# A graph layer on one core: first target scores fetched one a period, feature sums and residual moved to TensorE and ScalarE

## The chip, the cores and the metric

One core of one Trainium2 chip runs the kernel. The metric is the device time of one execution in microseconds (us), median of three runs. One execution was also recorded by the hardware profiler; all durations below come from that one.

## What is computed

Cut to what matters. `x` is 6250 x 256 in fp32, `src` and `dst` are 106250 edges sorted by target.

```python
xn = layernorm(x)
x = x + gnn(xn, src, dst) + mix(xn)
x = x + ffn(layernorm(x))            # 8 experts, softmax gate

def gat_conv(x, W, al, ar, src, dst):          # gnn: twice, 8 heads x 64, then 1 head x 256
    feat = x @ W;  el, er = feat . al, feat . ar
    e = leaky_relu(el[src] + er[dst], 0.2)
    alpha = exp(e - max over dst) / sum over dst
    return sum over dst of alpha * feat[src]

def mix(x):                                     # linear attention, 8 heads of 32
    q, k, v = elu(x Wq) + 1, elu(x Wk) + 1, x Wv
    context, k_sum = k^T v, sum of k
    return (q context / (q k_sum)) @ Wproj + bproj
```

elu(u) + 1 is max(u, 0) + exp(-max(-u, 0)): a positive part and an exponential part. For the keys the kernel calls the sum of the two parts `kphi`.

## The kernel before

The program runs five passes one after the other: the node pass (normalise, project, write the table of rows for layer one), the index pass, the edge pass of layer one, the hidden pass (ELU and the second projection), and the edge pass of layer two. `edge_pass` is one function, called with `L1` and the side work `Mixing`, then with `L2` and the side work `Experts`.

**The edge pass** cuts the edges, in order of target, into 52 blocks of 16 steps of 128 edges; four blocks form a group (13 groups), and each of the 128 lanes walks 64 consecutive edges per group. For each step GpSimd's queue (POOL) issues an indirect DMA that gathers 128 rows of the source nodes (2080 bytes each in layer one), L1349. In layer one there are two buffers of 16 steps, so the gather of step g of block n waits until VectorE (DVE) has summed step g of block n-2. In layer two there are three buffers. ScalarE (ACT) scales four of the eight heads of a step (L1486, four instructions a step), DVE the other four in one instruction a block (L1430). Then DVE adds step after step to a running sum, L1463, one 128x512 instruction a step in layer one. Each waits for the step before it. The softmax weights of block n+1 (`head`, L1402 to L1421) are worked out by DVE ahead of step 12 of block n in layer one, ACT takes their exponential (L1477, L1479, semaphore `wr_ready`) behind its last step of block n, and DVE's L1430 of block n+1 waits for it. Two rings of sums are stored to memory by SyncE's queue (SP), 1 MB each, after steps 8 and 16. In block 0 of each group the tails of the lanes of the last group are joined (class `Tails`), which makes that block longer.

**The scores of the targets** (`er`) are loaded per group. The first edge of each lane has its score fetched by its own indirect DMA, `first_er(q)`, L1339: the one of group 0 at the start, the other twelve in a run in block `n == B` (block 2 in layer one, block 3 in layer two), one ahead of each step's gather. At the very start POOL fetches `er_ali`, waits until it has landed, writes it to `starts` (L1334), and only then issues `first_er(0)` and the first gathers. SP's loads of `er` wait for that write.

**The side work of layer one**, class `Mixing`, is hung on the steps of the edge pass. In blocks 0 to 25 (the first half) two tiles of 121 nodes a block, t0 and t1, are projected by TensorE (`project`, L975 and L978, into the PSUM tiles p_kv and p_q). ACT makes the exponential parts of keys and queries behind its steps 4 and 11 (`exponents`, L941 to L945, tile `low`). DVE copies the values (L876, `vext`), adds up the keys' parts (L878, `kphi`) and the queries' parts (L880, into `nd_feat`, semaphore `q_kept`) ahead of steps 6 and 13. TensorE adds keys times values to the context (`context`, L986). TensorE's order is written out in `tensor`: project t0, context t0, project t1, context t1. `project` of a tile waits for `q_kept` of the tile before it.

In blocks 26 to 51 (the second half) the queries are weighed by the context (`weigh`, L1000 and L1001), DVE divides ahead of steps 2 and 8 (`quotient`, L902 to L906), TensorE transposes the result (`turn_back`, L1008), ACT copies it behind its steps 4 and 10 (`turn`, L951), TensorE projects it (`output`, L1016 and L1018, semaphore `o_ready`), and DVE adds the input row x ahead of steps 6 and 12 (`residual`, L915). TensorE's order is weigh t0, turn back t0, output t0, weigh t1, turn back t1, output t1. SP stores the result and loads the row of two tiles later.

The POOL queue's order and its one wait, around which a part of the change is made:

```python
for n in range(NB):
    for g in range(G):
        if n == B and 1 <= g < Q:
            first_er(g)
        wait(pool, summed, (n - B) * G + g + 1)
        nc.gpsimd.indirect_dma_start(out=rows[:, n % B, g, :], ...)
```

## Time and profile before

| | |
|---|---|
| median of 3 runs | 3355.85 us (3355.46 to 3357.4) |
| the profiled execution's own time | 3355.96 us |
| its span, first to last instruction | 3353.5 us, so 2.5 us lie around it |
| busy: PE, DVE, ACT, POOL | 2061.7, 2423.0, 1879.5, 2147.9 us |
| share of busy time: PE, DVE, ACT, POOL | 61%, 72%, 56%, 64% |
| mean granted TensorE clock | 0.752 of full speed |
| edge pass of layer one | from about 303 to 1645 us |
| edge pass of layer two | from about 1920 us to the end |

The shares are averages over passes with different limits, so each pass is read on its own. Engines: PE is TensorE's matmuls, PEld its weight loads, DVE is VectorE, ACT is ScalarE, POOL is GpSimd, SP is SyncE. A clock of 1.0 is 2.4 GHz, 0.5 is 1.2 GHz. An idle time in a row is that of the engine just before the instruction, with what ended it. Most instructions overlap the next by a part of their duration, so the cost of one in a row of them is the distance from start to start. A matmul in fp32 is two instructions in the profile. Matmul rows name output, moving operand, and stationary operand in the order out<-moving,stationary. A row of busy time by stretch has the stretch from and to in us from the span's start, its length, the busy us (and instructions) of PE, PEld, DVE, ACT and POOL, the granted clock, the mean busy share of the 16 DMA engines, and the GB/s that they moved. A row of a timeline has the start, the us, engine, line, operation, tiles, shapes, how many were merged (xN), and in brackets the idle time before them with what ended it.

### The profile page before, as it was taken

How to read it: one execution, taken by the hardware profiler on the slowest of the kernel's cores; microseconds unless marked ns; L12 is line 12 of the kernel's file. 1: busy time of each engine (PE TensorE's matmuls, PEld its weight loads, DVE VectorE, ACT ScalarE, POOL GpSimd, SP SyncE). 2: the span in 40 equal slices, each digit the busy share in tenths (PEclk: the TensorE clock that was granted, in tenths of full speed). 3: DMA queues.
4: the chain of work that ended last, by engine and by line, in shares of the span. 5: the costliest groups of instructions: out<-in, count | busy, mean ns of one | idle time of the engine just before them, and what ended most of it. 6: DMA issues, size and time to landing. Idle time of an engine off the chain costs nothing. (4 is left out here: it accounts for less than half of the span.)

```text
span 3353.5 us, 33809 instructions
## 1 busy us (share of the span) xinstructions
PE 2061.7 (61%) x6977; PEld 1301.7 (39%) x6977; DVE 2423.0 (72%) x6006; ACT 1879.5 (56%) x6177; POOL 2147.9 (64%) x2067
## 2 busy tenths in 40 slices
PE   6800354455545544444456500389999999999999
PEld 5600233333323322332244300255555555555565
DVE  6881799999988888888778535566666676767632
ACT  3400687777877766676544322456566566656632
POOL 2326777767666767676277577777777777777300
PEclk9955666666665555555588855699999999999999
DMA  7512899999999999999665357666666666666400
GB/s 232 138 22 82 277 368 346 354 351 360 348 350 344 366 352 367 346 366 365 258 169 147 85 170 246 197 188 207 206 207 208 217 217 205 201 205 207 156 26 12
DMA packets 249060, 793.61 MB, mean 237 GB/s; under 512 B 72064, under 2 KB 120035, under 8 KB 222197
## 3 DMA queue, kind: packets, MB, share of 16 engines
q0 software_dynamic: 132448, 379.32, 36.3%
q1 hardware_dynamic: 86327, 391.15, 30.7%
q10 hardware_dynamic: 30078, 20.99, 2.5%
q8 instruction: 56, 0.92, 0.1%
q14 instruction: 151, 1.24, 0.1%
HBM read 414.03 MB, written 378.16 MB: 236 GB/s over the span
## 5 line engine op out<-in xcount | busy, mean ns | idle before, releaser
L1349 POOL DMA_INDIRECT e_rows<-scratch_table,k_src x1664 | 1716.4, 1031 | 643.9 <-issue 347.9
L1486 ACT ACTIVATE e_rows<-e_rows,e_wr 128x64 f32<-128x64 f32 (+1 forms) x4160 | 1186.2, 367 | 3.4
L1463 DVE SCALAR_TENSOR_TENSOR e_ring<-e_ring,e_kext,e_rows 128x512 f32<-128x512 f32 (+1 forms) x1560 | 958.8, 615 | 239.1 <-ACT e_rows L1486 151.1
L2123 PE MATMUL e_p_y<-e_wfo,e_h 128*121 128x256 f32 x1664 | 394.1, 392 | 41.4 <-DVE e_y L1885 41.3
L2123 PEld LDWEIGHTS e_p_y<-e_wfo,e_h 128*121 128x121 f32 x1664 | 314.5, 191 | 139.6 <-ACT e_h L2032 66.5
L2109 PE MATMUL e_p_b<-e_h,e_wf 128*128 128x484 f32 x832 | 359.7, 575 | 10.6 <-ACT e_h L2032 10.6
L2097 PE MATMUL e_p_a<-e_xt,e_wf 128*128 128x484 f32 x832 | 357.6, 573 | 0.7 <-ACT e_xt L2047 0.7
L2032 ACT ACTIVATE e_h<-e_p_a,e_shift,e_scale 128x484 f32<-128x484 f32 x208 | 155.3, 752 | 269.6 <-PE e_p_a L2097 269.6
L986 PE MATMUL e_p_c<-e_vext,e_kphi 121*128 121x129 f32 x208 | 63.9, 462 | 310.2 <-DVE e_kphi L878 310.2
L1885 DVE SCALAR_TENSOR_TENSOR e_y<-e_p_y,e_w,e_y 121x256 f32<-121x256 f32 x416 | 180.3, 475 | 102.4 <-PE e_p_y L2123 102.3
L1430 DVE TENSOR_TENSOR e_rows<-e_rows,e_shared 128x4096 f32<-128x4096 f32 x52 | 229.6, 4416 | 15.4 <-ACT e_wr L1479 15.4
L2109 PEld LDWEIGHTS e_p_b<-e_h,e_wf 128*128 128x128 f32 x832 | 154.3, 191 | 178.5 <-issue 171.3
L2097 PEld LDWEIGHTS e_p_a<-e_xt,e_wf 128*128 128x128 f32 x832 | 157.6, 191 | 146.4 <-issue 140.9
L1008 PE MATMUL e_p_q<-k_ident,e_low 121*128 121x121 f32 x104 | 34.5, 434 | 291.8 <-DVE e_low L906 291.8
L2032 ACT ACTIVATE e_h<-e_p_b,e_shift,e_scale 128x484 f32<-128x484 f32 x208 | 152.6, 749 | 87.9 <-PE e_p_b L2109 86.1
L975 PE MATMUL e_p_kv<-e_wkv,nd_feat 128*121 128x512 f32 x208 | 184.2, 1041 | 0.0
L986 PEld LDWEIGHTS e_p_c<-e_vext,e_kphi 121*128 121x128 f32 x208 | 48.5, 323 | 318.5 <-DVE e_kphi L878 318.5
L1008 PEld LDWEIGHTS e_p_q<-k_ident,e_low 121*128 121x128 f32 x104 | 16.2, 215 | 297.0 <-DVE e_low L906 297.0
L951 ACT COPY e_att_t<-e_p_q 128x242 f32<-128x242 f32 x52 | 18.8, 362 | 182.0 <-PE e_p_q L1008 182.0
L1682 PE MATMUL hi_p_f<-hi_w,hi_ht 128*121 128x272 f32 x416 | 120.2, 439 | 0.0
L1016 PE MATMUL e_p_c<-e_wproj,e_att_t 128*121 128x256 f32 x208 | 105.8, 662 | 18.1 <-ACT e_att_t L951 18.1
L218 POOL DMA_INDIRECT na_found<-in_dst,na_piece x52 | 54.8, 1054 | 94.7 <-DVE na_piece L270 94.7
(406 smaller groups left out, 3466.7 us busy)
## 6 DMA issues: line engine op xcount, KB each, us to landing
scratch_sums<-e_ring SPq DMA_DIRECT2D x104, 2112.0 KB
scratch_sums<-e_ring SPq DMA_DIRECT2D x104, 1032.0 KB
e_rows<-scratch_table,k_src POOLq DMA_INDIRECT x1664
scratch_table<-na_frow ACTq DMA_DIRECT2D x52, 245.8 KB
scratch_table<-hi_frow ACTq DMA_DIRECT2D x52, 124.8 KB
na_x<-in_x SPq DMA_DIRECT2D x13, 484.0 KB
...
```

What stands on the lines that cost most here:

```text
L975: nc.tensor.matmul(self.p_kv[0:BK, :], self.k.feat[:, t, kt, :], self.wkv[:, kt, :], start=kt == 0, stop=kt == 1)
L986: last = nc.tensor.matmul(self.p_c[:, m * (P + 1):(m + 1) * (P + 1)], self.kphi[:, m * P:(m + 1) * P], self.vext[:, m, :], start=False, st ...
L1349: nc.gpsimd.indirect_dma_start(out=rows[:, n % B, g, :], out_offset=None, in_=table, in_offset=bass.IndirectOffsetOnAxis(ap=k.src[:, n * G ...
L1430: c(nc.vector.tensor_tensor(v, v, broad(share(b)[:, AH:H, 1:G1].rearrange("p h j -> p j h"), dim), ALU.mult))
L1463: nc.vector.scalar_tensor_tensor(ring[:, i, j - c0, 0:W], prev, kext[:, 0, j + 1:j + 2], rows[:, rb, j, 0:W], ALU.mult, ALU.add).then_inc( ...
L1486: last = nc.scalar.activation(rows[:, rb, j, at], rows[:, rb, j, at], ACT.Copy, scale=wr[:, b, h, j + 1:j + 2])
L1682: last = nc.tensor.matmul(p_f[b][0:BK, 0:D + 16], ht[:, b, kt, :], w2[:, kt, :], start=kt == 0, stop=kt == 3)
L1885: last = nc.vector.scalar_tensor_tensor(y, self.p_y[bank][0:BK, i % 2 * D:(i % 2 + 1) * D], self.w[:, i, e:e + 1], y, ALU.mult, ALU.add)
L2032: self.nc.scalar.activation(h[:, e % 2, mt, :], p[mt][:, 0:GN], ACT.Relu, bias=self.shift[:, layer, 2 * e + mt:2 * e + mt + 1], scale=self ...
L2097: last = nc.tensor.matmul(self.p_a[mt][:, 0:GN], self.wf1[:, e, kt, mt * P:(mt + 1) * P], self.xt[:, kt, :], start=kt == 0, stop=kt == 1)
L2109: last = nc.tensor.matmul(self.p_b[mt][:, 0:GN], self.wf2[:, e, kt, mt * P:(mt + 1) * P], self.h1[:, e % 2, kt, :], start=kt == 0, stop=kt ...
L2123: last = nc.tensor.matmul(self.p_y[bank][0:BK, i * D:(i + 1) * D], self.h2[:, e % 2, kt, v:v + BK], self.wfo[:, e, kt, :], start=kt == 0, ...
```

## The change

Three parts.

- POOL's order, both layers: `first_er(0)` and two gathers are issued ahead of the wait for `er_ali` and its write to `starts`. The other twelve first scores are fetched one a group, at step 8 of block 1 of the group before.
- First half of layer one: DVE no longer copies the values nor adds the keys' parts. ACT copies the values (`vext`) and writes the keys' positive part (`kphi`, now without the exponential part), and `context` multiplies both parts, `kphi` and `low`, with the values: four matmuls for two. ACT releases the context (`phi_ready`) itself.
- Second half: TensorE adds the input row x by a product with the identity, ahead of the projection, into the same PSUM tile. ACT copies the result behind its steps 7 and 13, DVE has no `residual`.

```diff
     def features(self, dve, t):
         nc, k = self.nc, self.k
-        dve.wait_ge(self.projected, t + 1)
-        wait(dve, self.ctx_added, t)
         if t == NB - 1:
+            dve.wait_ge(self.ctx_added, t)
             nc.vector.tensor_scalar(self.vext[:, :, P:P + 1], k.iop[0:BK, :].unsqueeze(1).to_broadcast([BK, 2, 1]),
-                                    float(NODES - t * BK), None, ALU.is_lt)
-        nc.vector.tensor_copy(self.vext[:, :, 0:P], self.p_kv[0:BK, D:2 * D].rearrange("p (m v) -> p m v", m=2))
+                                    float(NODES - t * BK), None, ALU.is_lt).then_inc(self.masked, 1)
         dve.wait_ge(self.exp_ready, t + 1)
-        nc.vector.scalar_tensor_tensor(self.kphi[:, :], self.p_kv[0:BK, 0:D], 0.0, self.low[0:BK, 0:D],
-                                       ALU.max, ALU.add).then_inc(self.phi_ready, 1)
         nc.vector.scalar_tensor_tensor(k.feat[:, t, :, :].rearrange("p m v -> p (m v)"), self.p_q[:, 0:2 * BK], 0.0, self.low[:, D:D + 2 * BK],
                                        ALU.max, ALU.add).then_inc(self.q_kept, 1)

-    def residual(self, dve, t):
-        nc = self.nc
-        dve.wait_ge(self.o_ready, t + 1)
-        dve.wait_ge(self.x_in[t % 2], t // 2 * 16 + 16)
-        wait(dve, self.res_out[t % 2], t // 2 * 16)
-        nc.vector.tensor_tensor(self.res[:, t % 2, :], self.p_c[0:BK, 0:D], self.x[:, t % 2, :],
-                                ALU.add).then_inc(self.res_ready, 1)
+    def residual(self, act, t):
+        act.wait_ge(self.o_ready, t + 1)
+        wait(act, self.res_out[t % 2], t // 2 * 16)
+        self.nc.scalar.copy(self.res[:, t % 2, :], self.p_c[0:BK, 0:D]).then_inc(self.res_ready, 1)

     def exponents(self, act, t):
         nc = self.nc
         act.wait_ge(self.projected, t + 1)
+        wait(act, self.ctx_added, t)
         wait(act, self.q_kept, t)
         nc.scalar.activation(self.low[0:BK, 0:D], self.p_kv[0:BK, 0:D], ACT.Relu, scale=-1.0).then_inc(self.low_ready, 1)
         nc.scalar.activation(self.low[:, D:D + 2 * BK], self.p_q[:, 0:2 * BK], ACT.Relu, scale=-1.0).then_inc(self.low_ready, 1)
+        nc.scalar.copy(self.vext[:, :, 0:P], self.p_kv[0:BK, D:2 * D].rearrange("p (m v) -> p m v", m=2))
+        nc.scalar.activation(self.kphi[:, :], self.p_kv[0:BK, 0:D], ACT.Relu)
         act.wait_ge(self.low_ready, 2 * t + 2)
-        nc.scalar.activation(self.low[0:BK, 0:D], self.low[0:BK, 0:D], ACT.Exp, scale=-1.0)
         nc.scalar.activation(self.low[:, D:D + 2 * BK], self.low[:, D:D + 2 * BK], ACT.Exp, scale=-1.0
                              ).then_inc(self.exp_ready, 1)
+        nc.scalar.activation(self.low[0:BK, 0:D], self.low[0:BK, 0:D], ACT.Exp, scale=-1.0).then_inc(self.phi_ready, 1)

     def context(self, pe, t):
         nc = self.nc
         pe.wait_ge(self.phi_ready, t + 1)
+        if t == NB - 1:
+            pe.wait_ge(self.masked, 1)
         for m in range(2):
-            last = nc.tensor.matmul(self.p_c[:, m * (P + 1):(m + 1) * (P + 1)], self.kphi[:, m * P:(m + 1) * P],
-                                    self.vext[:, m, :], start=False, stop=False, skip_group_check=True)
+            for part in (self.kphi, self.low):
+                last = nc.tensor.matmul(self.p_c[:, m * (P + 1):(m + 1) * (P + 1)], part[0:BK, m * P:(m + 1) * P],
+                                        self.vext[:, m, :], start=False, stop=False, skip_group_check=True)

     def output(self, pe, t):
         nc = self.nc
+        wait(pe, self.res_ready, t)
+        pe.wait_ge(self.x_in[t % 2], t // 2 * 16 + 16)
+        nc.tensor.matmul(self.p_c[0:BK, 0:D], self.k.ident[0:BK, 0:BK], self.x[:, t % 2, :], start=True, stop=False)
         pe.wait_ge(self.att_kept, t + 1)
-        wait(pe, self.res_ready, t)
         for m in range(2):
             nc.tensor.matmul(self.p_c[0:BK, 0:D], self.att_t[:, m * BK:(m + 1) * BK], self.wproj[:, m, :],
-                             start=m == 0, stop=False)
+                             start=False, stop=False)

         @block.gpsimd
         def _(pool):
...
-            pool.wait_ge(ali_in, 16)
-            nc.gpsimd.indirect_dma_start(
-                out=starts, out_offset=bass.IndirectOffsetOnAxis(ap=k.ali_row[:, 0:1], axis=0),
-                in_=er_ali[:, 0:EW], in_offset=None, bounds_check=P * T - 1, oob_is_err=False).then_inc(ali_out, 16)
...
             first_er(0)
             for n in range(NB):
                 for g in range(G):
-                    if n == B and 1 <= g < Q:
-                        first_er(g)
+                    if n == 0 and g == 2:
+                        pool.wait_ge(ali_in, 16)
+                        nc.gpsimd.indirect_dma_start(
+                            out=starts, out_offset=bass.IndirectOffsetOnAxis(ap=k.ali_row[:, 0:1], axis=0),
+                            in_=er_ali[:, 0:EW], in_offset=None, bounds_check=P * T - 1, oob_is_err=False).then_inc(ali_out, 16)
+                    if n % PB == 1 and g == G // 2 and n // PB + 1 < Q:
+                        first_er(n // PB + 1)
                     wait(pool, summed, (n - B) * G + g + 1)
```

`Mixing.vector` loses its two calls of `residual`, `Mixing.scalar` has them behind steps 7 and 13; the semaphores of the first scores alternate by group (`er0_in[q % 2]`).

How the order moves. POOL at the start of the edge pass of layer one, before (e_er stands for the tile of the first scores, e_rows for that of the gathered rows):

```order
L1331 DMA e_er_ali<-scratch_er,k_ali_dst 13x8
L1334 DMA scratch_starts<-e_er_ali,k_ali_row 106496x8
L1339 DMA e_er<-scratch_er,k_dst 128x8
L1349 DMA e_rows<-scratch_table,k_src 128x520 x33
L1339 DMA e_er<-scratch_er,k_dst 128x8
```

and with the change:

```order
L1332 DMA e_er_ali<-scratch_er,k_ali_dst 13x8
L1336 DMA e_er<-scratch_er,k_dst 128x8
L1351 DMA e_rows<-scratch_table,k_src 128x520 x2
L1345 DMA scratch_starts<-e_er_ali,k_ali_row 106496x8
L1351 DMA e_rows<-scratch_table,k_src 128x520 x22
L1336 DMA e_er<-scratch_er,k_dst 128x8
L1351 DMA e_rows<-scratch_table,k_src 128x520 x64
L1336 DMA e_er<-scratch_er,k_dst 128x8
```

The write to `starts` has gone behind two gathers, and the first scores of the next groups come once in 64 gathers.

TensorE in one block of the second half, before (L1008 turns back, L1016 and L1018 are the output, L1000 and L1001 weigh the next tile):

```order
L1008 MATMUL e_p_q<-k_ident,e_low 128x121 x2
L1016 MATMUL e_p_c<-e_wproj,e_att_t 121x256 x2
L1018 MATMUL e_p_c<-e_bproj,e_one 121x256
L1000 MATMUL e_p_kv<-e_cbd,nd_feat 121x128
L1001 MATMUL e_p_kv<-e_ksum,nd_feat 121x4
```

and with the change:

```order
L1007 MATMUL e_p_q<-k_ident,e_low 128x121 x2
L1014 MATMUL e_p_c<-e_wkv,k_ident 121x256
L1017 MATMUL e_p_c<-e_wproj,e_att_t 121x256 x2
L1019 MATMUL e_p_c<-e_bproj,e_one 121x256
L999 MATMUL e_p_kv<-e_cbd,nd_feat 121x128
L1000 MATMUL e_p_kv<-e_ksum,nd_feat 121x4
```

A matmul of 256 columns (L1014; e_wkv is where the row x lies) stands between the transposes and the projection, ahead of the weighing of the next tile.

## Rows read from the trace of the kernel before

**Rows 1.** Busy time by stretch: first half, second half, layer two.
```profile
620.00:1000.00 380.00, 188.94 (x522) 117.45 (x520) 346.27 (x638) 299.29 (x1208) 269.50 (x245) 0.65 0.95 351
1080.00:1560.00 480.00, 227.16 (x652) 145.11 (x652) 423.12 (x821) 330.21 (x1365) 328.02 (x303) 0.51 0.96 361
2400.00:2770.00 370.00, 350.31 (x1161) 209.01 (x1160) 257.79 (x820) 225.12 (x516) 282.85 (x287) 0.98 0.68 209
```
**Rows 2.** Timeline of POOL, start of layer one (start, us, what, idle before).
```profile
303.77 0.90 POOL L1331 DMA_INDIRECT e_er_ali<-scratch_er,k_ali_dst  x1 [7.24 <-POOLq L114]
306.68 0.91 POOL L1334 DMA_INDIRECT scratch_starts<-e_er_ali,k_ali_row  x1 [2.01 <-DMA e_er_ali<-scratch_er,k_ali_dst]
352.84 0.94 POOL L1339 DMA_INDIRECT e_er<-scratch_er,k_dst  x1 [0.30 <-issue]
```
**Rows 3.** Timeline of DVE, same stretch: its waits for gathered rows.
```profile
358.65 0.39 DVE L1402 TENSOR_TENSOR e_z<-e_rows,e_er 128x128 f32<-128x128 f32 x1 [6.07 <-DMA e_rows<-scratch_table,k_src]
391.49 0.46 DVE L1402 TENSOR_TENSOR e_z<-e_rows,e_er 128x128 f32<-128x128 f32 x1 [10.22 <-DMA e_rows<-scratch_table,k_src]
```
**Rows 4.** Waits of POOL in layer two, 1900 to 3200: total, times, longest.
```profile
POOL e_rows L1349 <- issue: 190.4, 625, 0.3
...
POOL scratch_starts_b L1334 <- DMA e_er_ali<-scratch_er,k_ali_dst: 2.2, 1, 2.2
```
**Rows 5.** Busy time of blocks 12 and 14; sums of blocks 12-15 and 32-35.
```profile
645.72:672.15 26.43, 11.54 (x37) 7.34 (x37) 25.13 (x51) 22.50 (x92) 18.87 (x17) 0.69 0.94 336
...
695.78:719.83 24.05, 12.11 (x33) 7.56 (x32) 22.43 (x46) 19.20 (x79) 13.63 (x13) 0.64 0.86 322
...
sum 99.00, PE 50.23 PEld 31.30 DVE 90.20 ACT 78.31 POOL 67.57; mean PE 12.56 PEld 7.83 DVE 22.55 ACT 19.58 POOL 16.89
...
sum 102.79, PE 48.12 PEld 30.55 DVE 90.66 ACT 70.68 POOL 64.81; mean PE 12.03 PEld 7.64 DVE 22.67 ACT 17.67 POOL 16.20
```
**Rows 6.** Timeline of DVE, block 14.
```profile
706.65 0.40 DVE L876 COPY e_vext<-e_p_kv 121x256 f32<-121x256 f32 x1
...
707.30 0.40 DVE L880 SCALAR_TENSOR_TENSOR nd_feat<-e_p_q,e_low 128x242 f32<-128x242 f32 x1
...
715.77 0.75 DVE L1463 SCALAR_TENSOR_TENSOR e_ring<-e_ring,e_kext,e_rows 128x512 f32<-128x512 f32 x1 [0.83 <-ACT e_rows L1486]
...
717.42 2.49 DVE L1463 SCALAR_TENSOR_TENSOR e_ring<-e_ring,e_kext,e_rows 128x512 f32<-128x512 f32 x3
```
**Rows 7.** Timeline of TensorE, block 14.
```profile
707.44 1.23 PE L986 MATMUL e_p_c<-e_vext,e_kphi 121*128 121x129 f32 x4 [8.05 <-DVE e_kphi L878]
708.46 3.62 PE L975 MATMUL e_p_kv<-e_wkv,nd_feat 128*121 128x512 f32 x4
711.87 1.48 PE L978 MATMUL e_p_q<-nd_feat,e_wq 128*128 128x121 f32 x8
```
**Rows 8.** Timeline of ACT, block 14.
```profile
713.39 0.38 ACT L941 ACTIVATE e_low<-e_p_kv 121x256 f32<-121x256 f32 x1 [4.76 <-PE e_p_q L978]
...
714.69 3.91 ACT L1486 ACTIVATE e_rows<-e_rows,e_wr 128x64 f32<-128x64 f32 x16
```
**Rows 9.** Timeline of DVE, block 34.
```profile
1215.79 0.42 DVE L915 TENSOR_TENSOR e_wkv<-e_p_c,e_wkv 121x256 f32<-121x256 f32 x1 [0.97 <-PE e_p_c L1018]
1217.85 0.14 DVE L902 TENSOR_SCALAR e_den<-e_p_kv 121x8 f32<-121x8 f32 x1
```
**Rows 10.** Timeline of TensorE, block 34.
```profile
1212.55 2.06 PE L1016 MATMUL e_p_c<-e_wproj,e_att_t 128*121 128x256 f32 x4 [0.45 <-ACT e_att_t L951]
1214.55 1.21 PE L1018 MATMUL e_p_c<-e_bproj,e_one 1*121 1x256 f32 x2
1215.68 0.78 PE L1000 MATMUL e_p_kv<-e_cbd,nd_feat 128*121 128x128 f32 x2
...
1217.09 0.42 PE L1001 MATMUL e_p_kv<-e_ksum,nd_feat 128*121 128x4 f32 x2
```
**Rows 11.** Timeline of ACT, block 34.
```profile
1219.45 0.36 ACT L951 COPY e_att_t<-e_p_q 128x242 f32<-128x242 f32 x1 [0.82 <-PE e_p_q L1008]
```

14 lines of the change are left out of this document (7 added, 7 removed).

## The prediction

> **What bounds the kernel now.** I read the busy time by stretch first, to see which passes the change touches and what is near its limit there. In both halves of layer one DVE is busy 91% and 88% of the time and the DMA engines 95% and 96%, at 351 and 361 GB/s; TensorE has slack, and its clock stands mostly at its lower level, 1.2 GHz (granted 0.65 and 0.51) [rows 1]. In layer two neither is full. There POOL is: its waits are 625 gaps of 0.3 us with the releaser "issue", none longer, and one single wait of 2.2 us at the start [rows 4]; 287 indirect DMAs in 370 us are one each 1.29 us [rows 1]. So layer two costs what POOL has to issue, whatever the order.
>
> Then I read the blocks of layer one, which repeat in fours: 99.0 us in the first half, 102.8 us in the second [rows 5]. The same four blocks move some 34.7 MB and 37.1 MB (351 and 361 GB/s), and at a full share the engines would move 351/0.95 = 369 and 361/0.96 = 376 GB/s, so the transfers alone need 94.0 us and 98.7 us. That is a floor near by, but the view of waits names none of DVE in the two stretches that is for a transfer.
>
> Last I read the timelines, for what DVE waits for. In block 14 it is a loop over four engines. DVE adds the queries' parts (L880) and so releases `q_kept`; TensorE finishes context t0 and projects t1; ACT starts its exponents at 713.39, 5.69 us after L880 ended, and has waited 4.76 us for that [rows 6 to 8]. Four ACT instructions later come the rows, DVE waits 0.83 us for the first of them [rows 6], and ACT's weights for the next block are just ready when DVE gets there at 719.83 [rows 5]. The reader is to see that DVE is 91% busy and yet paced by this loop.
>
> **Part one, the order of POOL.** In layer one POOL waited 2.01 us for `er_ali` [rows 2]; with three indirect DMAs in between (1.25 us each) that has landed, and only the usual 0.3 us gap is left: -1.7 us, since DVE's first weights wait for the sixteenth gather. The twelve first scores stood in a run from 352.84 on [rows 2], each ahead of one gather, and DVE then waited 10.22 us for the rows of block 2 [rows 3]. Twelve less one at 1.25 us are 13.75 us, more than the wait, so it goes: -10.2 us. Next late would be DVE itself. SP's loads of `er` start 3 us later, hidden by the 16 gathers. The wait of 6.07 us in block 0 [rows 3] stays. In layer two the count of DMAs is the same and POOL never rests, so only the wait of 2.2 us, less its gap, is saved: -1.9 us. The run there cost DVE a wait too, but DVE only gets a lead that POOL takes back by 1.25 us a group. Bounds: -3.6 us if the rows of block 2 are late for another reason, -19.9 us if the wait in block 0 goes too. Sum: -13.8 us.
>
> **Part two, the first half.** From L876 to L880 in start times are two instructions, 0.65 us [rows 6]. They leave DVE twice a block: 1.3 us. But in blocks like 14 the loop decides:
> - L880 comes 0.65 us earlier: -0.65.
> - Context t0 leaves the way to project t1, since ACT now releases it long before. It stood there from 707.44 to 708.46, while `q_kept` came at 707.70, so 0.76 us [rows 6, 7]. Without its run-in TensorE may do the eight short products (1.48 us, some of them at 2.4 GHz) at 1.2 GHz throughout, up to 0.4 us more: I take -0.45.
> - ACT gets a copy and a relu between 713.39 and the rows at 714.69, where four take 1.30 us [rows 8]. Two more are 0.65 at most; less where the wait between relus and exponentials is now covered: +0.5. The row of ACT's added ones is that of its neighbours, as no row shows the copy from PSUM by itself.
> - The four rows behind them take ACT 3.91 us, 0.98 each [rows 8]; DVE takes 0.83 for a sum [rows 6]. So ACT leads the end of the block and DVE's second 0.65 us is mostly lost.
>
> That is -0.6 us for each of two blocks in four. In block 12 and its like the joining of the tails makes DVE's part longer (26.43 us) [rows 5] and ACT waits little: the full -1.3. In the last of four ACT keeps a copy of the sums after DVE's last step: -0.65 and a part of the second, -0.8. Four blocks: -3.3 us, to 95.7, above the 94 of the transfers. Blocks 3 to 25 are 23: 23/4 x 3.3 = **-19 us**. The doubled context (four fp32 products, 1.0 us more, TensorE idle 8.05 us before it [rows 7]) lies outside the loop. Bounds: 0, when ACT's two instructions cost 0.65 and TensorE gives nothing (the loop then still keeps -0.65 of DVE, which DMA at its floor could eat), and 5 us of four blocks down to the transfers' 94, -29.
>
> **Part three, the second half.** DVE loses `residual`: 0.34 us for t1, and for t0 the wait, 0.97 us in block 34 [rows 9]. But what follows it there is `quotient` t1 at 1217.85, and that needs the weighing of t1, which TensorE ended at 1217.51 [rows 9, 10]. So the wait was cover: DVE would only wait at L902 instead. And the identity product is put before it. Two passes of 256 columns cost what two of L1016's four do, 1.0 us of 2.0 [rows 10]; 0.45 us of it fits in the gap in which TensorE waits for ACT's copy [rows 10], so the weighing ends 0.55 us later, at 1218.1, and L902 0.3 us later. ACT's copy of the result (0.36, as [rows 11] by shape) waits for `o_ready` behind step 7, holds steps 8 to 10, and makes the turn of t1 some 0.5 us later than 1219.45, where ACT had 0.82 us of slack [rows 11]. The 0.34 us of t1 pays the 0.3 back. In the two blocks in four where the tails' products stand in that gap the identity product shows in full, +0.1 and +0.4. Four blocks: +0.5; over 26 blocks +3 us, and some of it comes back where the longer stretch of TensorE's work raises its clock. I take **0**. No row shows the product or the copy itself, so the bounds: -1.0 us a block (all DVE instructions and waits gone, down to the transfers' 98.7 us a four), -27 us, and +0.5 us a block, +13.
>
> **The sum** against the profiled execution's own 3355.96 us (0.1 above the median): -13.8 - 19 + 0 = -32.8, so **3323 us**.
>
> **Rivals.**
> - TensorE speeds up. For it: output and weighing, 4.96 us from 1212.55 to 1217.51, get the identity product where the gap was, and with the transposes ahead of it become one unbroken stretch of over 6 us [rows 10]; against it: the clock is 0.51 in a half that already has 4.96 [rows 1]. If it does, it is in the weighing, at the end of the stretch. Its 1.83 us (1215.68 to 1217.51) then halve, L902 comes 0.45 us earlier than before, and with the 0.34 that is -0.8 us x 26 = -21: 3302 us. Chance 0.2. The Trainium skill ("TensorE: Matmul & The Clock Gate", What's actually happening) says that activity releases the clock, the default being the lower one; by that rule the change would come out here, and the higher clock of the first half, where the unbroken stretch is 5.9 us (707.44 to 713.35) [rows 7], agrees.
> - DVE was the bound. Its instructions and its short waits all count: first half down to the transfers (23/4 x 5 = -29), second too (-27): 3356 - 14 - 56 = 3286 us. For it the 91%, against it the waits behind both. Chance 0.12.
> - Mixing gives nothing: ACT's two instructions at full price, TensorE's project slower by what the context left, and the +3 us of the second half. Then only POOL's order counts, 3342 to 3345 us. Chance 0.13. This is also the case that the moved work isn't the moved bound.
> - Slower. ACT and TensorE take turns in series in the second half: identity product 1.0, the wait for `o_ready` behind step 7 1.0 and the copy 0.36, all on the way to the turn of t1, less none: 2.4 us a block, +62, with -33 elsewhere: 3385 us. It decides from 1.3 us a block on (33/26). The 0.82 of ACT's slack [rows 11] speaks against it. Chance 0.04.
>
> **How the numbers follow.** The forecast has 0.5 with 3308 to 3340 as its own range (-29 or -9 in the first half, -8 to +10 in the second). Rivals: 0.2, 0.12, 0.13, 0.04, and 0.01 for none. From 3290 to 3343 leaves out the DVE rival, the slow one and a bit of the third. A measurement of this kernel can tell 0.2%, 6.7 us, from no change. Faster by more: 0.5 + 0.2 + 0.12 and most of 0.13, 0.93; within: 0.04; slower: 0.03.
>
> **What would show it.** The wait of 10.22 us gone and block 1 near 23 us instead of 33; four blocks of the first half near 95.7 us, with DVE still waiting for ACT; in the second half near 103, with a new wait of DVE at L902 for the weighing, 1 us or more, where that at L915 was; a clock above 0.6 there would be the first rival. Layer two from its start to its end shorter by 2 us alone. If DVE begins to wait for gathered rows in the middle of layer one, the transfers have become the bound; if four blocks of the second half take over 108 us, the slow rival holds.

## The result, and the profile after

The changed kernel takes **3304.92 us** (median of four runs, 3300.46 to 3307.29), the kernel before 3356.62 beside it (3355.46 to 3359.66): ratio **0.984**, 95% interval 0.983 to 0.986. That is 51.7 us less, where 33 were forecast; the range held it. In the two profiled executions the span went from 3353.5 to 3305.5 us, 48.0 less.

Where they went is read from the starts of the first big DVE instruction of each block of layer one (L1430 before, L1432 after), 52 in each trace:

| stretch | before, us | after, us | difference | forecast |
|---|---|---|---|---|
| up to layer one's first weights | 336.3 | 335.0 | -1.3 | -1.7 |
| block 0 | 28.7 | 28.3 | -0.4 | 0 |
| block 1 | 32.9 | 22.3 | -10.6 | -10.2 |
| block 2 | 24.5 | 23.3 | -1.2 | 0 |
| blocks 3 to 25 | 570.5 | 540.6 | -29.9 | -19 |
| second half, from block 26 | 644.3 | 635.5 | -8.8 | 0 |
| from the last block's start to the end | 1716.4 | 1720.5 | +4.2 | -1.9 |

Busy time by stretch of the changed kernel, the stretches of [rows 1] shifted by what the kernel gained (columns as there):

```profile
600.00:980.00 380.00, 207.29 (x674) 130.55 (x674) 343.53 (x629) 324.57 (x1324) 288.06 (x261) 0.70 0.98 368
1040.00:1520.00 480.00, 229.80 (x735) 151.66 (x733) 417.90 (x793) 348.91 (x1429) 337.73 (x311) 0.57 0.97 366
2350.00:2720.00 370.00, 347.67 (x1160) 210.37 (x1160) 250.84 (x796) 218.44 (x501) 283.25 (x285) 0.98 0.66 207
```

DVE is still busy 90% of the first half; ACT rose from 79% to 85%, the DMA share from 0.95 to 0.98, TensorE's granted clock from 0.65 to 0.70 and in the second half from 0.51 to 0.57. The blocks that answer to [rows 5], 12 to 15, with their sum, 94.4 us instead of 99.0:

```profile
619.69:645.30 25.61, 11.24 (x37) 7.00 (x37) 23.89 (x47) 22.56 (x94) 20.12 (x19) 0.73 0.98 361
645.30:667.96 22.66, 14.51 (x45) 8.79 (x44) 20.01 (x33) 18.25 (x75) 16.82 (x16) 0.73 1.00 378
667.96:690.37 22.41, 12.87 (x42) 8.13 (x41) 21.24 (x42) 20.02 (x83) 17.32 (x17) 0.68 0.97 366
690.37:714.13 23.76, 13.39 (x42) 8.23 (x41) 20.02 (x32) 20.65 (x83) 18.49 (x17) 0.69 1.00 390
sum 94.44, PE 52.02 PEld 32.15 DVE 85.16 ACT 81.48 POOL 72.76; mean PE 13.01 PEld 8.04 DVE 21.29 ACT 20.37 POOL 18.19
```

The waits of DVE from block 1 to the end of layer one (for whom, us in total, times, longest):

```profile
DVE e_ring L1465 <- ACT e_rows L1488: 40.7, 110, 1.1
DVE e_den L898 <- PE e_p_kv L1000: 31.6, 23, 3.4
DVE e_rows L1432 <- ACT e_wr L1481: 13.5, 12, 1.1
```

The wait of 10.22 us [rows 3] is gone. The wait for the output (29.2 us, 25 times in the same view of before) is gone as well, and 31.6 us, 23 times, for the weighing (L898) stand in its place (L898 is L902 of before). No wait for a transfer is named, although the DMA share is 0.98.

The loop of block 14, which [rows 6 to 8] show before, now in DVE, TensorE and ACT:

```profile
679.63 3.38 PE L971 MATMUL e_p_kv<-e_wkv,nd_feat 128*121 128x512 f32 x4 [2.99 <-DVE nd_feat L876]
682.85 1.05 PE L974 MATMUL e_p_q<-nd_feat,e_wq 128*128 128x121 f32 x8
685.78 0.70 PE L985 MATMUL e_p_c<-e_vext,e_kphi 121*128 121x129 f32 x2 [1.88 <-ACT e_low L938]
```
```profile
683.94 0.38 ACT L931 ACTIVATE e_low<-e_p_kv 121x256 f32<-121x256 f32 x1 [2.36 <-PE e_p_q L974]
...
685.29 0.44 ACT L938 ACTIVATE e_low<-e_low 121x256 f32<-121x256 f32 x1
685.60 3.92 ACT L1488 ACTIVATE e_rows<-e_rows,e_wr 128x64 f32<-128x64 f32 x16
```

The queries' sum (L876) ends at 679.57 and ACT starts its exponents at 683.94: 4.37 us, where it was 5.69. The contexts of t0 lie before it, from 674.55 to 676.64. From the exponents to the rows are 1.66 us (1.30 before).

### The profile page after: what moved, and what is told of

The parts are those of the page before. It is cut to its first block and busy times, and to the rows that moved or that the text cites. A ratio compares the mean times of both kernels' runs of the same rounds, so it can differ in the third digit from the quotient of the medians.

```text
span 3305.5 us, 34381 instructions
## 1 busy us (share of the span) xinstructions
PE 2097.6 (63%) x7289; PEld 1329.7 (40%) x7289; DVE 2371.6 (72%) x5850; ACT 1917.2 (58%) x6333; POOL 2158.8 (65%) x2067
## 5 line engine op out<-in xcount | busy, mean ns | idle before, releaser
L2111 PE MATMUL e_p_b<-e_h,e_wf 128*128 128x484 f32 x832 | 365.7, 583 | 21.8 <-ACT e_h L2034 21.8
L1887 DVE SCALAR_TENSOR_TENSOR e_y<-e_p_y,e_w,e_y 121x256 f32<-121x256 f32 x416 | 180.1, 474 | 102.3 <-PE e_p_y L2125 102.3
L1432 DVE TENSOR_TENSOR e_rows<-e_rows,e_shared 128x4096 f32<-128x4096 f32 x52 | 229.7, 4417 | 15.5 <-ACT e_wr L1481 15.4
L971 PEld LDWEIGHTS e_p_kv<-e_wkv,nd_feat 128*121 128x121 f32 x208 | 58.0, 309 | 176.1 <-DVE nd_feat L876 121.8
L381 PE MATMUL na_p_f<-na_w,nd_feat 128*121 128x264 f32 x416 | 105.5, 398 | 8.3 <-ACT nd_feat L341 8.2
```

The lines of the kernel that those rows point to most:

```text
L381: last = nc.tensor.matmul(p_f[b][h][0:BK, 0:D + 8], k.feat[:, n, kt, :], w1[:, kt, h, :], start=kt == 0, stop=kt == 1)
L971: nc.tensor.matmul(self.p_kv[0:BK, :], self.k.feat[:, t, kt, :], self.wkv[:, kt, :], start=kt == 0, stop=kt == 1)
L1432: c(nc.vector.tensor_tensor(v, v, broad(share(b)[:, AH:H, 1:G1].rearrange("p h j -> p j h"), dim), ALU.mult))
L1887: last = nc.vector.scalar_tensor_tensor(y, self.p_y[bank][0:BK, i % 2 * D:(i % 2 + 1) * D], self.w[:, i, e:e + 1], y, ALU.mult, ALU.add)
L2111: last = nc.tensor.matmul(self.p_b[mt][:, 0:GN], self.wf2[:, e, kt, mt * P:(mt + 1) * P], self.h1[:, e % 2, kt, :], start=kt == 0, stop=kt ...
```

## The experiments

Single parts were timed on four further chips: pool, first, second and l2burst on one, after_again, first_again, noident and ctxlate on the next, before_again, pool_again and halftraffic on the third, zeroprod on the last. On all of them the kernel before takes 3655 to 3663 us, not 3356, so each run is set against before by its ratio on its own chip. The unchanged changed kernel ran on the first chip and on the second of these (after_again), and no part ran on the first chip. Lengths of blocks are read from each trace as above. They can still be compared: in both runs of pool nearly every block after the first three has the length that it has in before on the first chip, to 0.1 us. In the other runs some blocks are 3 to 10 us longer than others of their kind, and I call the rest undisturbed. "Kind" is the place in the four: the first joins the tails. All runs in one table; "rest" is from the start of layer one's last block to the end:

| run | median, us | ratio to before (95%) | block 0 | 3 to 25 | 26 to 50 | rest |
|---|---|---|---|---|---|---|
| before (first chip) | 3356.6 | | 28.7 | 570.5 | 644.3 | 1716.4 |
| changed (first chip) | 3304.9 | 0.984 (0.983-0.986) | 28.3 | 540.6 | 635.5 | 1720.5 |
| before_again | 3655.1 | 1.000 (0.998-1.002) | 56.0 | 583.3 | 661.0 | 1972.0 |
| after_again | 3622.6 | 0.991 (0.989-0.994) | 38.2 | 585.8 | 653.8 | 1958.9 |
| pool | 3608.7 | 0.984 (0.982-0.987) | 39.9 | 569.8 | 644.3 | 1968.8 |
| pool_again | 3592.1 | 0.982 (0.979-0.984) | 39.4 | 569.8 | 644.8 | 1949.3 |
| first | 3663.8 | 1.000 (0.998-1.001) | 55.4 | 583.4 | 660.2 | 1981.0 |
| first_again | 3658.1 | 1.001 (0.999-1.002) | 56.3 | 579.3 | 657.6 | 1961.9 |
| second | 3674.2 | 1.002 (1.000-1.004) | 56.7 | 589.8 | 666.7 | 1981.8 |
| l2burst | 3640.0 | 0.995 (0.992-0.997) | 39.3 | 583.7 | 672.3 | 1958.4 |
| noident | 3610.0 | 0.987 (0.984-0.989) | 38.8 | 582.8 | 641.1 | 1960.5 |
| ctxlate | 3622.3 | 0.990 (0.987-0.992) | 38.1 | 574.0 | 658.3 | 1971.9 |
| halftraffic | 3637.2 | 0.993 (0.991-0.995) | 27.4 | 587.3 | 669.6 | 1961.5 |
| zeroprod | 3631.4 | 0.993 (0.991-0.995) | 39.2 | 596.2 | 659.2 | 1955.7 |

**pool**: the kernel before with POOL's order alone.

```diff
-                    if n == B and 1 <= g < Q:
-                        first_er(g)
+                    if n % PB == 1 and g == G // 2 and n // PB + 1 < Q:
+                        first_er(n // PB + 1)
```

(and the store of `er_ali` behind two gathers, as in the change).

> The kernel before with POOL's new order alone. The prediction on record says -13.8 us, 3342 us. Read from the changed kernel's trace (block 1 shorter by 10.6 us, layer one's first weights 1.25 us earlier, but layer two 4.5 us longer where I had it 1.9 shorter) there are two theories. One: layer two's 4.5 us belong to the new order (the first scores now stand among the gathers of the whole pass), then this run is only 7 to 9 us faster than before and its layer two is near 1438 us instead of 1433. Rival: they are scatter of the single DMAs between executions, then 12 to 14 us faster. Either way blocks 12 to 15 stay near 99.0 us and blocks 32 to 35 near 102.7, and the wait of 10.22 us for the rows of block 2 is gone.

Measured: 54.5 us faster, four times what the larger of the two theories said, so it decides between neither. Blocks 12 to 15 take 99.0 us as expected. What I had not counted on are block 0, the long blocks and what lies behind layer one, see before_again.

**first**: the kernel before with the first half's part alone.

```diff
+        nc.scalar.copy(self.vext[:, :, 0:P], self.p_kv[0:BK, D:2 * D].rearrange("p (m v) -> p m v", m=2))
+        nc.scalar.activation(self.kphi[:, :], self.p_kv[0:BK, 0:D], ACT.Relu)
...
+            for part in (self.kphi, self.low):
```

> The kernel before with the part of the first half alone (ScalarE copies values and keeps the keys' relu, TensorE adds the two feature parts). The prediction on record says -3.3 us for four blocks, 95.7 us, and -19 in all. My theory from the changed kernel's trace: TensorE's share of the loop was mis-sized (from q_kept to ScalarE's exponents 4.37 us instead of 5.69), so four blocks take 94.3 to 94.8 us, the whole is 27 to 31 us faster, some 3327 us, and this holds without the other two parts. Rival: part of the 30 us came from POOL's order (the gathers ahead), then four blocks take 95.5 to 96.5 here and the whole is 17 to 21 us faster. Blocks 32 to 35 stay near 102.7 us by both.

Measured: no difference in the whole, 1.000, and 1.001 in its repetition. But the undisturbed blocks of the four kinds take 25.6, 22.0, 23.4 and 23.7 us (medians of those of a kind), 94.7 together, against 26.4, 23.6, 24.1 and 24.9 in before. Of the third kind only one of five is undisturbed; the other four take 28.1 to 34.3 us. So the loop's saving is there without POOL's order in single blocks, 4.3 us in four of them, as my theory said, and in this chip's whole it does not show: blocks 3 to 25 take 583.4 us, though at 94.7 they would need 545. Blocks 32 to 35, 28.4 with 24.6, 24.6 and 25.0, are those of before, so the second half owes nothing to the first.

**second**: the kernel before with the second half's part alone.

```diff
+        nc.tensor.matmul(self.p_c[0:BK, 0:D], self.k.ident[0:BK, 0:BK], self.x[:, t % 2, :], start=True, stop=False)
...
+        self.nc.scalar.copy(self.res[:, t % 2, :], self.p_c[0:BK, 0:D]).then_inc(self.res_ready, 1)
```

> The kernel before with the part of the second half alone (the identity product, ScalarE copies the result). The prediction on record says 0, between -8 and +10. The changed kernel's trace has the second half 8.8 us shorter. Theory: that is this part's own work, the identity product costing next to nothing since it falls in TensorE's gap, so this run is 7 to 11 us faster and blocks 32 to 35 take 100 to 101.5 us. Rival: the second half only got a better start from the first (its transfers were further ahead), then this run is within 3 us of before, with the four blocks near 102.7. In the first half blocks 12 to 15 stay at 99.0.

Measured: 11 us slower by the medians, which the interval (1.000 to 1.004) does not tell from nothing. Many of its blocks are long ones. The shortest of each kind in the second half (27.8, 24.5, 24.1, 24.8) sum to 101.2, inside what the theory said, but the medians don't (29.0, 26.0, 24.1, 24.8, together 103.8): not settled by this run.

**l2burst**: the changed kernel with the old run of first scores in layer two alone.

```diff
-                    if n % PB == 1 and g == G // 2 and n // PB + 1 < Q:
-                        first_er(n // PB + 1)
+                    if L is L1:
+                        if n % PB == 1 and g == G // 2 and n // PB + 1 < Q:
+                            first_er(n // PB + 1)
+                    elif n == B and 1 <= g < Q:
+                        first_er(g)
```

> The changed kernel, but in layer two the twelve first scores stand in a run again at block 3. If the spread ones cost layer two its 4.5 us, this run is 4 to 7 us faster than the changed kernel (some 3299 us, layer two near 1432 us). If it is scatter or the durations of POOL's issues, it is within 2 us of the changed kernel, 3305 us, and layer two is again near 1438.

Measured: the rest takes 1958.4 us, that of the changed kernel on such a chip 1958.9. No cost of the order shows there. But the rest differs by 19.5 us between the two runs of pool, so 4 us could not show in it, and POOL rests there: its gathers of layer two have 467.9 us of idle time before them in pool and 253.5 in before. This run can't settle what cost the first chip 4.2 us.

**after_again**, **first_again**: the changed kernel and the first part, unchanged, on the next chip.

> The changed kernel once more, as the control for the three beside it, since the chip of the first four runs took 3663 us for the kernel before, where the first one took 3356, with engines standing for up to 10 us with the releaser issue. If this chip is like the first (before at some 3356 us), 3301 to 3307 us and blocks 12 to 15 at 94.4 us. If it is like the other (before at some 3660 us), the theory that instructions and stores come late there whatever the order says 3600 to 3645 us, the rival that its order of transfers matters says as slow as before, 3660.

> The part of the first half alone, as in the run named first. On a chip like the first: my theory says four blocks of the first half at 94.3 to 94.8 us and 27 to 31 us faster than before, the rival (POOL's order gave a share of it) 95.5 to 96.5 us and 17 to 21 us faster. On a chip like the other one: within 0.2% of before again, since standing engines give the saved time back.

The changed kernel keeps 35 of its 52 us there. first_again repeats first: 1.001, with undisturbed blocks of 25.6, 21.8, 23.3 or 24.0, and 23.5 us.

**ctxlate**: the changed kernel with one wait more.

```diff
         pe.wait_ge(self.phi_ready, t + 1)
+        pe.wait_ge(self.q_kept, t + 1)
```

> The changed kernel with one wait added: TensorE's context of a tile waits for q_kept of the same tile too, so context t0 stands between q_kept and project t1 again. Theory (the loop DVE, TensorE, ScalarE sets blocks 13 and 14 and their like, and the context was 1 to 1.4 us of it): each of these two takes 0.7 to 1.6 us more, four blocks 96 to 97.5 us instead of 94.4, and the whole is 9 to 18 us slower than the changed kernel. Rival (DVE or the transfers set the pace in the changed kernel, DMA share 0.98): within 3 us of it, four blocks at 94.4 to 94.8.

In the whole no difference from after_again (long blocks hide it: 3 to 25 are even shorter by 11.8 us). The undisturbed blocks show it. Blocks 13 to 15 by stretch:

```profile
670.47:693.84 23.37, 12.73 (x45) 8.57 (x44) 20.04 (x33) 20.52 (x84) 16.38 (x15) 0.72 0.97 358
693.84:717.94 24.10, 12.00 (x43) 7.37 (x42) 21.31 (x41) 20.13 (x82) 17.89 (x17) 0.71 0.96 360
717.94:742.59 24.65, 12.76 (x42) 8.34 (x41) 20.06 (x33) 20.65 (x84) 18.13 (x17) 0.64 0.97 358
```

They are 0.7, 1.7 and 0.9 us longer than in the changed kernel, 3.3 in four blocks with the 25.6 of the first kind unchanged: 97.7, a little over the theory's 96 to 97.5. Two whole fours without a long block, 4 to 7 and 16 to 19, take 98.9 and 98.7 us where the changed kernel takes 94.4 and 93.3 and before 99.3 and 99.0, so the one wait gives back nearly all of the first half's gain in them. DVE's busy time is the same and the DMA share is 0.96 to 0.97, under the changed kernel's 0.97 to 1.00: neither DVE's work nor the transfers set these blocks. TensorE in block 14 of this run, to be held against the three lines above:

```profile
705.62 0.77 PE L986 MATMUL e_p_c<-e_vext,e_kphi 121*128 121x129 f32 x2 [8.08 <-DVE nd_feat L876]
...
707.47 3.12 PE L971 MATMUL e_p_kv<-e_wkv,nd_feat 128*121 128x512 f32 x4
710.43 1.05 PE L974 MATMUL e_p_q<-nd_feat,e_wq 128*128 128x121 f32 x8
```

The context delays the projection by 1.85 us (705.62 to 707.47) and gives back only 0.26 in its first products (3.12 against 3.38).

**noident**: the changed kernel without the identity product.

```diff
-        nc.tensor.matmul(self.p_c[0:BK, 0:D], self.k.ident[0:BK, 0:BK], self.x[:, t % 2, :], start=True, stop=False)
```

> The changed kernel without the identity product: the input row isn't added, so the computation lacks the residual there; its load and TensorE's wait for it stay. By the price of my prediction (0.55 us a block on the path, two blocks in four more) this is 10 to 14 us faster than the changed kernel and blocks 32 to 35 take 97.5 to 98.5 us. By the theory from the changed kernel's trace (the product's 0.85 us lie nearly whole in TensorE's gap: the projection starts 1.31 us after the turn where it started 1.11 before, and its bias comes 0.16 us sooner) it is 0 to 4 us faster and four blocks take 99 to 99.7 us. If the product also raises the clock of what follows it, it may even be 1 to 3 us slower.

This kernel leaves the input row out of the result. Its undisturbed blocks take 28.5, 24.8, 24.1 and 24.8 us, 102.2 together, no less than the mean of the changed kernel on the first chip, which is 635.5 / 25 x 4 = 101.7. So by single blocks the product costs nothing net, and not the 99 to 99.7 of the theory either. It is not free everywhere: block 29 of the changed kernel takes 25.7 us against 24.8, both at a granted clock of 0.50, for there the tails' products fill the gap, and the output product starts 3.45 us behind the turn with the identity product and 2.46 without it.

The whole can't confirm this. On its own chip this run is 12.7 us faster than after_again, inside the 10 to 14 us of my prediction's price. All of it stands in the first two blocks of the fours, 7.9 and 5.5 us, and the first ones of after_again are longer than on the first chip by something else: in block 28 (30.0 us) DVE goes on at L898 2.83 us after TensorE's weighing has ended, where on the first chip it goes on at once. The second ones, 25.0 to 26.5 against 24.3 to 25.2, are likely the product's own cost.

In block 32 it even helps. TensorE there from the turn of t1 on, changed kernel first, then this one:

```profile
1121.71 0.65 PE L1007 MATMUL e_p_q<-k_ident,e_low 121*128 121x121 f32 x2
1122.14 0.93 PE L1014 MATMUL e_p_c<-e_wkv,k_ident 121*121 121x256 f32 x2
1122.91 1.03 PE L1017 MATMUL e_p_c<-e_wproj,e_att_t 128*121 128x256 f32 x4
1123.87 0.69 PE L1019 MATMUL e_p_c<-e_bproj,e_one 1*121 1x256 f32 x2
```
```profile
1180.29 0.67 PE L1007 MATMUL e_p_q<-k_ident,e_low 121*128 121x121 f32 x2 [0.52 <-issue]
1181.49 2.04 PE L1016 MATMUL e_p_c<-e_wproj,e_att_t 128*121 128x256 f32 x4 [0.54 <-ACT e_att_t L943]
1183.46 1.21 PE L1018 MATMUL e_p_c<-e_bproj,e_one 1*121 1x256 f32 x2
```

From 1113.70 on the changed kernel's TensorE has no gap, and its output products take half the time, those of the higher level of the clock. With the gaps of 0.33, 0.52 and 0.54 us it stays at the lower one. In blocks 28 to 43 of noident the granted clock is 0.50 in all but block 33 (0.57); in the changed kernel eleven of the sixteen are above it, up to 0.71.

**before_again**, **pool_again**, **halftraffic**: what the long blocks are. halftraffic is the changed kernel with this:

```diff
+            if L is L1:
+                nc.vector.memset(rows[P // 2:P, :, :, :], 0.0)
...
-                    nc.gpsimd.indirect_dma_start(out=rows[:, n % B, g, :], ...
+                    nc.gpsimd.indirect_dma_start(out=rows[0:h, n % B, g, :], ...
```

(`h` is 64 in layer one.)

> The kernel before, unchanged, to have its trace from a chip on which it takes some 3660 us instead of 3356. From the traces of its parts there (first, second, first_again) my theory says: block 0 of layer one takes 55 to 57 us (28.7 on the first chip), since the twelve first scores in a run stand before gathers that are slower there; blocks that no standing engine lengthens take 26.4, 23.6, 24.1 and 24.9 us as on the first chip; but some blocks take 3 to 10 us more, 20 to 40 us in all, and layer two takes some 1965 us from layer one's end. Rival: it is as undisturbed as the run named pool, with layer one at some 1317 us (1301 and 16 more in block 0), then the other 35 us are in layer two.

> POOL's new order alone, once more. In the first run of it no block after the first was longer than on the first chip (99.0 and 102.7 us for four blocks, layer one 1301 us) and it was 55 us faster than before, 14 us faster than the whole change was on such a chip. Theory: a program whose engines need the full DMA share less often (0.95 against 0.98 in the changed kernel) is spared the standing engines, so it repeats: 3600 to 3615 us. Rival: how instructions and stores happen to fall decides, then this run has long blocks as the others do and takes 3620 to 3650 us. POOL's order saves at least the 16 us of block 0 by both.

> The changed kernel, but layer one gathers rows for 64 of the 128 partitions alone; the other half is zero, so sums and scores of those partitions leave out the gathered rows. Same number of DMAs, a quarter less moved in layer one. Theory (the long blocks come from DMA engines at their full share, behind which instructions and stores come late; blocks without them are set by DVE and ScalarE): no blocks longer by 3 us or more, four blocks of the first half at 94 to 95 us, of the second at 99.5 to 101.5, layer one 1240 to 1260 us. Rival (transfers set the pace in all blocks of the changed kernel, also on the first chip): four blocks fall below 93 and 99 us. Second rival (engines stand on this chip whatever is moved): long blocks as before, layer one over 1300 us.

before_again: block 0 takes 56.0 us and 39.4 in pool_again, so there the run of first scores costs 16.6 us in block 0 (on the first chip 10.6, in block 1). On the first chip DVE waited for gathers, here it doesn't: L1463 waits in block 0, 26.2 us in six waits, for which the view names an old load of the node pass; in the code it waits for ACT's scaled rows. Four blocks are long, 16, 22, 36 and 43. Two of them:

```profile
760.05:791.95 31.90, 11.12 (x37) 7.23 (x36) 25.19 (x50) 22.66 (x91) 20.37 (x20) 0.66 0.84 302
1468.19:1502.36 34.17, 11.61 (x33) 7.35 (x33) 21.61 (x40) 16.36 (x65) 23.27 (x24) 0.50 0.90 337
```

DVE's and ACT's busy time in them is that of other blocks; they stand. Together with smaller ones that is 29.7 us more than in pool_again, which again has none at all: blocks 3 to 25 take 569.8 us in both of its runs. 16.6 + 29.7 and 22.7 in the rest (the rest differs by 19.5 us between the two runs of pool) are its gain there, in the spans. So the long blocks belong to the program on these chips, for four of them repeat in place and size (blocks 15 or 16, 22, 36 and 43 in before_again, first_again and second), and pool has none. halftraffic refutes my theory for them: with 254 GB/s and a DMA share of 0.77 in the first half, by the first line below, where after_again has 339 and 0.92, it has as many of them as after_again, 587.3 us in blocks 3 to 25 against 585.8 (its zeros delay the layer's start by 12 us, which its whole time holds). The second rival holds. The first falls too: its undisturbed blocks (25.6, 22.7 or 21.6, 22.3 or 23.2, 23.4 or 23.8) are those of the changed kernel, so the transfers do not set them. Nor do they set block 0: it is 27.4 us for 38.2, but it starts 12.1 us later (346.5 for 334.4) and ends at the same time (373.9 for 372.6).

```profile
620.00:1000.00 380.00, 197.42 (x620) 124.57 (x620) 312.56 (x547) 305.36 (x1223) 249.84 (x238) 0.68 0.77 254
1100.00:1600.00 500.00, 237.01 (x728) 154.84 (x728) 408.11 (x776) 344.81 (x1402) 319.22 (x303) 0.55 0.79 264
```

What stands in a long block of after_again, block 12: timeline of ACT, scaling gathered rows.

```profile
660.04 0.58 ACT L1488 ACTIVATE e_rows<-e_rows,e_wr 128x64 f32<-128x64 f32 x2
661.40 0.35 ACT L1488 ACTIVATE e_rows<-e_rows,e_wr 128x64 f32<-128x64 f32 x1 [0.77 <-issue]
662.12 0.35 ACT L1488 ACTIVATE e_rows<-e_rows,e_wr 128x64 f32<-128x64 f32 x1 [0.38 <-issue]
663.53 0.35 ACT L1488 ACTIVATE e_rows<-e_rows,e_wr 128x64 f32<-128x64 f32 x1 [1.06 <-issue]
664.22 0.35 ACT L1488 ACTIVATE e_rows<-e_rows,e_wr 128x64 f32<-128x64 f32 x1 [0.35 <-issue]
```

The same in block 0 of that run, where ACT has no such gaps on the first chip:

```profile
351.45 0.41 ACT L936 ACTIVATE e_low<-e_low 128x242 f32<-128x242 f32 x1 [6.64 <-DMA scratch_er<-nd_er]
354.94 0.35 ACT L1488 ACTIVATE e_rows<-e_rows,e_wr 128x64 f32<-128x64 f32 x1 [1.05 <-issue]
356.33 0.35 ACT L1488 ACTIVATE e_rows<-e_rows,e_wr 128x64 f32<-128x64 f32 x1 [1.04 <-issue]
357.04 0.35 ACT L1488 ACTIVATE e_rows<-e_rows,e_wr 128x64 f32<-128x64 f32 x1 [0.36 <-issue]
```

In the code the scaling instructions wait for no semaphore once the block's weights are there, and yet they come one by one, in both places at some 0.7 or 1.4 us from start to start, while DVE waits for them, 4.03 us in block 12 and 11.15 in block 0. So block 0 is long for what makes the long blocks. It looks like instructions that arrive late, but no row shows what holds them, and I leave the cause open. "issue" alone is no proof of it: TensorE's idle time of 5.59 us before the context bears the releaser "issue" in pool_again and DVE in before, at the same length.

**zeroprod**: one product more, of zeros. (ident2, the same with the identity product itself issued twice, has no time.)

```diff
+        nc.tensor.matmul(self.p_c[0:BK, 0:D], self.zero[0:BK, 0:BK], self.x[:, t % 2, :], start=False, stop=False)
```

> The changed kernel with one more product of the same size behind the identity product, of zeros by the input row, so the result is the same. Without the identity product the blocks of the second half that no standing engine lengthened took 28.5, 24.8, 24.1 and 24.8 us (102.2 in four), with it 27.8, 23.9 or 25.6, 24.1 or 23.5, 24.7 or 23.9 (99.7 to 101.4), and TensorE's output and projection of block 32 fell from 2.04 and 1.21 us to 1.03 and 0.69. Theory (the product closes the gap in which TensorE waited, and the longer unbroken stretch brings the higher clock): with two products blocks 34 and 35 and their like get a granted clock above 0.6 (0.50 and 0.57 with one), and an undisturbed block is at most 0.3 us longer than with one. Rival (what fills more than the gap lies on the path): 0.4 to 0.8 us more in each block, four blocks 102 to 104.5 us.

Blocks 32 to 35:

```profile
1174.95:1203.62 28.67, 14.89 (x45) 10.10 (x45) 24.67 (x50) 21.61 (x88) 17.60 (x18) 0.56 0.94 350
1203.62:1230.29 26.67, 13.08 (x44) 8.51 (x44) 20.88 (x38) 15.51 (x65) 18.05 (x18) 0.63 0.94 339
1230.29:1255.21 24.92, 12.84 (x40) 9.09 (x40) 21.98 (x45) 18.52 (x77) 16.27 (x15) 0.57 0.92 343
1255.21:1280.80 25.59, 12.99 (x41) 8.99 (x41) 20.78 (x37) 18.50 (x74) 18.27 (x18) 0.57 0.98 372
sum 105.85, PE 53.80 PEld 36.69 DVE 88.31 ACT 74.14 POOL 70.18; mean PE 13.45 PEld 9.17 DVE 22.08 ACT 18.54 POOL 17.55
```

The rival holds in four of five fours: 28 to 47 sum to 105.6, 105.9, 106.4, 102.3 and 105.3, above even its 104.5. The clock did rise in block 34, from 0.50 to 0.57, but less than the theory asked, and that pays for nothing: the block is 0.8 us longer. The exception is 40 to 43, with 0.64 in its last three blocks, 25.1, 23.7 and 24.7 us. But blocks 30 and 31, at 0.71 and 0.70, take 24.5 and 25.1, longer than the changed kernel's at 0.50 (24.1 and 24.7). What the product adds, from the start of the turn to start of the output product in TensorE's timeline:

| | turn | next products | output product | us |
|---|---|---|---|---|
| without identity product (noident, block 34) | 1223.89 | | 1225.10 | 1.21 |
| changed kernel, block 34 | 1164.55 | 1165.01 | 1165.86 | 1.31 |
| with a second one (zeroprod, block 34) | 1238.64 | 1239.10, 1239.95 | 1240.81 | 2.17 |

The first product costs 0.10 us, the second 0.86. At the end of the weighing of t0 the first costs nothing: 6.12 us behind the start of the turn in the changed kernel, 6.13 in noident, 6.07 in before.

## Why the prediction was right, and where it was off

**Direction and range held**; the sum was 19 us too small (-33 against -51.7). 3304.9 lies below 3308 to 3340, the range of the forecast's own mechanism, and is in the stated range only by the room left for the rivals, so that the range held is in part luck. Of its 15.2 us of error in the spans, 10.9 stand in blocks 3 to 25 and 8.8 in the second half, against 6.1 the other way in layer two, and small terms.

**POOL's order in layer one: right.** -1.3, -0.4 and -10.6 us for -1.7, 0 and -10.2. The wait was pushed out by twelve DMAs less one, as said. pool_again shows the same order worth 16.6 us in block 0 on another chip, where DVE waits for ACT's rows and not for gathers, so that is no repetition of this mechanism.

**Layer two: the sign failed.** The wait of 2.2 us [rows 4] did go, and still the rest took 4.2 us more. What the views show is that POOL never rests over 0.3 us in either, but for the 2.2 us, and that its gathers there took longer each. The group of its gathers, after and before:

```profile
L1351 POOL DMA_INDIRECT e_rows<-scratch_table,k_src x832 | 817.1, 982 | 253.6 <-issue 191.7 <-DVE e_ring L1465 57.9 <-DVE e_ring L1445 4.0
```
```profile
L1349 POOL DMA_INDIRECT e_rows<-scratch_table,k_src x832 | 810.5, 974 | 253.5 <-issue 190.4 <-DVE e_ring L1463 59.7 <-DVE e_ring L1443 3.0
```

6.6 us in 832 gathers, where POOL paces the layer, less the 1.9 of the wait, is about the 4.2. Whether the new order makes them longer isn't settled. On the other chips one gather of layer two takes 982 and 983 ns with the old order (before_again, l2burst) and 983, 986 and 979 with the new (pool_again, pool, after_again), so nothing there shows that it does. The step that failed is "only the wait of 2.2 us, less its gap, is saved: -1.9 us": it took the price of one issue as fixed to 0.2%, which no row had shown.

**First half: mechanism right, one term above all mis-sized.** The loop from `q_kept` to ACT's exponents to the rows paced blocks like 14: after the change DVE waits for ACT's rows 68 times in blocks 3 to 25 instead of 17, and ctxlate makes the blocks longer by putting the context back. The three terms for block 14 were -0.65, -0.45 and +0.5, -0.6 in sum; the block shrank by 1.64 us. Term by term:

- The queries' sum was to end 0.65 us earlier. It ends 11.61 us behind the block's start instead of 11.92, only 0.31 earlier, since ACT with its two more instructions is late at the block's beginning:

```profile
675.76 0.75 DVE L1465 SCALAR_TENSOR_TENSOR e_ring<-e_ring,e_kext,e_rows 128x512 f32<-128x512 f32 x1 [0.26 <-ACT e_rows L1488]
```

- From there to ACT's exponents it is 4.37 us instead of 5.69, -1.32 where -0.45 was taken. This is the step that failed: "TensorE may do the eight short products (1.48 us, some of them at 2.4 GHz) at 1.2 GHz throughout, up to 0.4 us more: I take -0.45". It did the reverse: the project takes 4.27 us (679.63 to 683.90) where it took 4.89 [rows 7], the short products 1.05 instead of 1.48. The context that left the way did not take the clock with it. Its products now run earlier in the block, and there are twice as many; the granted clock of the block rose, 0.64 to 0.68.
- ACT's two instructions cost 0.36, not 0.5.
- From the rows to the next block's start it is 4.77 us instead of 5.14: 0.37 of DVE's second 0.65 us, which the prediction called mostly lost and put at nothing, are kept.

Together -1.64. The blocks 12 to 15 shrank by 0.8, 1.0, 1.6 and 1.1 us, where 1.3, 0.6, 0.6 and 0.8 were forecast, 4.6 for 3.3; so the term of the first kind was too large and hid a part of the error. Over blocks 3 to 25 it is 5.2 us in four.

The floor of 94.0 us for the transfers, which I gave as a bound, isn't one: blocks 8 to 11 and 16 to 19 of the changed kernel take 93.5 and 93.3 us, its block 5 moves 393 GB/s where the bound took 369 as the full rate, and halftraffic moves a quarter less and its undisturbed blocks are as long.

**Second half: one term mis-sized, and a rival at work in a part of it.** The step that failed is "so the weighing ends 0.55 us later": in blocks like 34 it ends 0.05 us later behind the turn than before. In the blocks of the tails the product shows in full, as the prediction said (block 29). Without it (noident) four blocks take 102.2 us, 0.5 less than before, which is DVE's lost addition and wait: some -3 us over the half, read across chips. The other 6 come most likely from the rival "TensorE speeds up", which I had given 0.2 and -21 us. It holds in part of the blocks only; its sign, a clock above 0.6 in the half, did not come (0.57). Blocks 28 to 31 of the changed kernel, at 0.50 in the last three, take 102.3 us, next to nothing gained; 32 to 35, at 0.71, 0.50 and 0.57 there, take 99.7. Single pairs of a kind: block 33 takes 23.9 us at 0.71 and 29 takes 25.7 at 0.50; 38 takes 23.5 at 0.57 and 34 takes 24.1 at 0.50; 35 takes 23.9 at 0.57 and 31 takes 24.7 at 0.50. Other pairs show nothing or the reverse: block 37 takes 25.6 at 0.57, as 29 does at 0.50, and 39 takes 25.1 at 0.57, more than 31. Blocks 29 and 33, the same work:

```profile
1030.03:1055.68 25.65, 14.39 (x40) 9.53 (x40) 20.69 (x38) 15.90 (x67) 17.72 (x16) 0.50 0.94 334
1132.30:1156.20 23.90, 9.50 (x40) 6.27 (x40) 20.73 (x38) 16.08 (x68) 16.81 (x16) 0.71 0.96 345
```

TensorE needs 9.50 us for what took it 14.39, and the block is 1.75 us shorter. That the higher clock is the cause and not a companion is likely from this and from block 32 of noident, but no run set the clock alone, and the other pairs say that it depends on where in the block the clock rises or on something else. The Trainium skill ("TensorE: Matmul & The Clock Gate", What's actually happening) says that activity releases the clock; by that rule the second half had to come out as the rival did, and the trace agrees for blocks like 33 and not for those at 0.50. In zeroprod, with one product more, the clock of block 34 rises as well, 0.50 to 0.57, and the block is longer all the same.

**The other rivals.** "DVE was the bound" (3286) falls: the changed kernel's DVE waits longer for ACT than before, 40.7 us against 23.8. "Mixing gives nothing" falls with the first half's 29.9 us. "ACT and TensorE in series" falls with the second half's 8.8 us less, where it asked for 62 more. The new wait at L898 that the prediction named as its own sign is there: 31.6 us, 1.4 on average where it asked for 1 us or more, in the place of the 29.2 us.

**What no step spoke of** is the other kind of chip. There POOL's order alone (0.982 to 0.984) beats the whole change (0.991), though on the first chip its fours are shorter, 93.3 to 94.4 and 99.7 to 102.3 against 99.0 to 99.3 and 102.5 to 103.2. Blocks 3 to 50 take 38.7 us less than before's on the first chip, and 25 us more than pool's on the others.
